# Second cross-attention of a Perceiver kernel: the context's transpose read back from DRAM, probabilities normalised ahead of transposing, context as the stationary operand, last key apart

## The reference, cut to what matters

```
def _L1_xattn_ref(queries, keys, values, mask, W_Q, W_K, W_V, W_O):
    B, S, D, H, DK, DV = (4, 256, 128, 16, 64, 64)
    b, skv, _ = keys.shape
    sq = queries.shape[1]
    scaling = 1.0 / DK ** 0.5
    Q = (queries @ W_Q).reshape(b, sq, H, DK)
    K = (keys @ W_K).reshape(b, skv, H, DK)
    V = (values @ W_V).reshape(b, skv, H, DV)
    scores = jnp.einsum('bqhd,bkhd->bhqk', Q, K)
    scores = jnp.where(mask == 0, -jnp.inf, scores)
    probs = jax.nn.softmax(scores * scaling, axis=-1)
    attn = jnp.einsum('bhqk,bkhd->bqhd', probs, V).reshape(b, sq, H * DV)
    return attn @ W_O
```

## Time and profile before

| | us |
|---|---|
| median of 3 runs | 2889.09 (2885.73 to 2889.99) |
| the profiled execution, its own time | 2895.22 |
| its span in the trace | 2893.4 |
| cross-attention 1: first query product to the last statistics | 1119.30 to 2015.25 |
| mean granted TensorE clock over the span | 0.908 of full speed |

### The profile page before, as it was taken

How to read it: one execution, slowest core, us unless ns; L and a number is a source line. 1 busy time by engine, 2 the same in 40 slices (tenths; PEclk the granted TensorE clock), 3 DMA queues, 4 the chain that set the end, 5 groups by cost and what they waited for, 6 DMA issues and landing times. The chain is left out here.

```text
span 2893.4 us, 70443 instructions
## 1 busy us (share of the span) xinstructions
PE 2370.2 (82%) x20920; PEld 1837.1 (63%) x20959; DVE 1764.7 (61%) x5309; ACT 1546.4 (53%) x3802; POOL 654.1 (23%) x1127
## 2 busy tenths in 40 slices
PE   5999999967649997999999999998256105479997
PEld 3777777745436666999999999997115103334444
DVE  5788788769844444656665666665798987521000
ACT  5888888844322224555555555554379638542221
POOL 2445454447513220111111111111000030000000
PEclk9999999989969997999999999998597655589999
DMA  3222222200000002111101011010000000010001
GB/s 89 74 75 71 73 74 74 60 3 0 19 5 0 0 0 59 32 29 29 30 27 30 27 30 30 28 27 23 13 0 0 0 0 4 0 41 0 0 0 29
DMA packets 150473, 79.92 MB, mean 28 GB/s; under 512 B 33504, under 2 KB 148592, under 8 KB 150128
## 3 DMA queue, kind: packets, MB, share of 16 engines
q1 hardware_dynamic: 150384, 78.77, 9.6%
HBM read 58.80 MB, written 19.92 MB: 27 GB/s over the span
## 5 line engine op out<-in xcount | busy, mean ns | idle before, releaser
L914 POOL TENSOR_TENSOR c_ON<-c_O,c_rden 128x512 f32<-128x512 f32 x128 | 133.4, 1042 | 718.4 <-DVE c_O L1091 718.4
L1077 DVE CUSTOM_DVE_ANT_0 c_SM<-c_bs,c_MB 128x257 f32<-128x257 f32 x512 | 215.1, 424 | 97.8 <-PE c_bs L941 95.9
L1036 ACT ACTIVATE c_OT<-c_bt 128x512 f32<-128x512 f32 x128 | 76.5, 597 | 367.2 <-PE c_bt L979 367.2
L952 PE MATMUL c_bo<-c_C,c_PT 128*128 128x128 f32 x2048 | 270.0, 275 | 0.3 <-ACT c_PT L1043 0.3
L941 PE MATMUL c_bs<-c_cT,c_QP 128*128 128x257 f32 x1024 | 266.5, 383 | 0.6 <-DVE c_cT L1059 0.5
L952 PEld LDWEIGHTS c_bo<-c_C,c_PT 128*128 128x128 f32 x2048 | 258.6, 192 | 7.3 <-ACT c_PT L1043 0.5
L666 ACT ACTIVATE a_PR<-a_SM,a_nmx 128x257 f32<-128x257 f32 x512 | 253.4, 499 | 4.0 <-issue 3.6
L1029 ACT ACTIVATE c_PR<-c_SM,c_nmx 128x257 f32<-128x257 f32 x512 | 253.6, 505 | 0.0
L713 DVE CUSTOM_DVE_ANT_0 a_SM<-a_bs,a_MB 128x257 f32<-128x257 f32 x512 | 188.0, 423 | 44.4 <-PE a_bs L534 38.5
L941 PEld LDWEIGHTS c_bs<-c_cT,c_QP 128*128 128x128 f32 x1024 | 175.9, 192 | 15.4 <-DVE c_cT L1059 0.9
L1099 DVE COPY c_PT<-c_bp 128x512 f32<-128x512 f32 x128 | 88.6, 692 | 132.8 <-PE c_bp L989 132.8
(11 more groups left out here) (479 smaller groups left out, 5722.0 us busy)
## 6 DMA issues: line engine op xcount, KB each, us to landing
a_C<-in_ctx_dram SPq DMA_DIRECT2D x128, 128.0 KB, 2.1
ctxT_dram<-a_cT SPq DMA_DIRECT2D x128, 128.0 KB, 1.9
c_C<-in_ctx_dram SPq DMA_DIRECT2D x128, 128.0 KB, 2.1
c_CL<-in_ctx_dram SPq DMA_DIRECT2D x128, 64.0 KB, 2.9
a_MK<-in_mask_Bx1xSxS_bk_dram SPq DMA_DIRECT2D x128, 32.1 KB, 1.9
X<-in_x_dram SPq DMA_DIRECT2D x4, 512.0 KB, 6.2
g_h<-in_L_ffn_h_w_dram SPq DMA_DIRECT2D x2, 1024.0 KB, 7.9
out_dram<-X SPq DMA_DIRECT2D x1, 2048.0 KB, 8.7
```

Source lines behind the costliest of these rows:

```text
L914: nc.gpsimd.tensor_tensor(ON[:, par, :, :], O1[:, :, :], bcast(rden[:, par, :], 2, D), ALU.mult).then_inc(on_ok, 1)
L952: last = nc.tensor.matmul(b_o[:, hg * D:(hg + 1) * D], PT[:, pair, i, c, :], C[:, (s.r - 2) % 8, c, :], start=(c == 0), stop=(c == 1))
L1077: nc.vector.tensor_tensor_reduce(SM[:, par, hg, :], b_s[hg % 2][:, 0:SK], MB[:, :], 1.0, NEG1, ALU.add, ALU.max, mx[:, par, hg:hg + 1]).th ...
```

## The change

- The transposed context is no longer made by TensorE and VectorE. SyncE loads it from `ctxT`, which cross-attention 0 has stored, into `cT`, now eight buffers deep, 128 KB for each element; the load of `CL` goes.
- VectorE multiplies the probabilities by the reciprocal of their sum, four instructions of 128x257 in place, ahead of the transposes. `ON`, its multiplication on GpSimd and its transposes go.
- The values are made with the context stationary and 512 columns of transposed probabilities moving: two products per element, which give the output already transposed; ScalarE copies it straight to `OT`.
- The 257th key is taken out of the values. GpSimd spreads its probabilities over a tile in `XL`; a small TensorE product with `fold` and a VectorE multiplication by `bmask` give `LT`; one more product, `LT` with `VB` (the last context rows through BH of each head), is accumulated to the output product. `VB` comes from a DRAM tensor that the preparation fills: four products of 512 columns, four ScalarE copies, one store of 1 MB.
- Scores have four banks instead of two and are issued together, ahead of the values. The small product and the output product write into spare columns of the banks `b_s[1]` and `b_s[0]`.

```
+            @block.sync
+            def _(sp):
+                sp.wait_ge(vb_ev, 4)
+                sp.dma_start(vb_dram, VBL[:, :, :]).then_inc(vb_out, 16)
+                sp.wait_ge(vb_out, 16)
...
+                pe.wait_ge(ab_ev, 8)
+                for c in range(4):
+                    wait(pe, vb_ev, c - 1)
+                    nc.tensor.matmul(b_pt[c % 2][:, :], sh.lastT[:, :], BH[:, 4 * c:4 * c + 4, :], start=True, stop=True
+                                     ).then_inc(vb_ps, 1)
...
         @block.sync
         def _(sp):
...
+            def step(s):
+                g, r = s.g, s.r
+                wait(sp, s_ps, 4 * (g - NC_ + 1))
+                sp.dma_start(cT[:, r, 0:LAST], sh.ctxT[ds(g, 1), :, :].rearrange("b d k -> d (b k)")
+                             ).then_inc(ct_in[r], 16)
+                wait(sp, av_ps, g - NC_ + 1)
                 sp.dma_start(C[:, r, :, :], ctx_rows[ds(g, 1), 0:LAST, :].rearrange("b (c p) d -> p (b c) d", p=P)
                              ).then_inc(c_in[r], 16)
-                sp.dma_start(CL[:, r, :], ctx_rows[ds(g, 1), LAST, :].broadcast_to([P, D])).then_inc(c_in[r], 16)
+                if r % 4 == 3:
+                    wait(sp, y_ps, s.tile - 1)
+                    sp.dma_start(VB[:, r // 4, :], vb_dram[ds(s.tile * BPT, BPT), :, :].rearrange("b h d -> (b h) d")
+                                 ).then_inc(vb_in[r // 4], 16)
...
# GpSimd
+                if s.on(1):
+                    wait(pool, n_ok, 4 * g)
+                    wait(pool, l_ps, s.fours(-1) - 1)
+                    nc.gpsimd.tensor_tensor(XL[:, (r - 1) // 4 % 2, (r - 1) % 4, :, :], bcast(sh.quarter[:, :], 1, 4),
+                                            PR[:, 1 - r % 2, :, LAST:SK].broadcast_to([P, 4, 4]), ALU.mult
+                                            ).then_inc(x_ok, 1)
...
# TensorE
+            def scores(s):
+                g, r = s.g, s.r
+                pe.wait_ge(ct_in[r], 16 * (s.eights(0) + 1))
+                wait(pe, last_cp, g + 1)
+                if r % 4 == 0:
+                    wait(pe, q_ev, 4 * (s.tile + 1))
+                for hg in range(4):
+                    wait(pe, s_mx, 4 * (g - 1) + hg + 1)
+                    if hg == 0 and r % 4 == 3:
+                        wait(pe, y_ev, s.fours(-7) + 1)
+                    if hg == 1 and r % 4 == 2:
+                        wait(pe, l_ev, s.fours(-6) + 1)
+                    nc.tensor.matmul(b_s[hg][:, 0:SK], QP[:, r // 4 % 2, r % 4, 4 * hg:4 * hg + 4, :], cT[:, r, :],
+                                     start=True, stop=True).then_inc(s_ps, 1)
+
+            def turn_probs(s, pair):
+                wait(pe, n_ok, 4 * (s.g - 1) + 2 * pair + 2)
+                wait(pe, (pt0_ev, pt1_ev)[pair], s.g - 1)
...
+            def values(s):
+                g, buf = s.g, (s.r - 2) % NC_
+                pe.wait_ge(c_in[buf], 16 * (s.eights(-2) + 1))
+                wait(pe, pt0_ev, g - 1)
+                wait(pe, pt1_ev, g - 1)
+                wait(pe, o_ev, g - 2)
+                for c in range(2):
+                    last = nc.tensor.matmul(b_o[:, :], C[:, buf, c, :], PT[:, s.r % 2, c, :, :],
+                                            start=(c == 0), stop=(c == 1))
+                last.then_inc(av_ps, 1)
 
             def step(s):
...
+                    scores(s)
                 if s.on(2):
+                    values(s)
                 if s.on(-4):
                     queries(s.tile + 1, r % 4)
+                if r % 4 == 1 and s.on(5):
+                    wait(pe, x_ok, 4 * s.fours(-5) + 4)
+                    if s.on(0):
+                        wait(pe, s_mx, 4 * g + 2)
+                    nc.tensor.matmul(b_s[1][0:BPT * H, SPARE:SPARE + SQ], XL[:, (r - 5) // 4 % 2, :, :, :],
+                                     sh.fold[:, :], start=True, stop=True).then_inc(l_ps, 1)
+                if r % 4 == 2 and s.on(6):
...
+                    for h in range(H):
+                        nc.tensor.matmul(b_s[0][:, SPARE:SPARE + D], OT[:, tp, h, :, :], BH[:, h, :],
+                                         start=(h == 0), stop=False)
+                    nc.tensor.matmul(b_s[0][:, SPARE:SPARE + D], LT[:, :, :], VB[:, tp, :], start=False, stop=True
+                                     ).then_inc(y_ps, 1)
                 if s.on(1):
+                    turn_probs(s, 0)
+                    turn_probs(s, 1)
...
# VectorE
                 if s.on(0):
...
                         nc.vector.tensor_tensor_reduce(SM[:, par, hg, :], b_s[hg][:, 0:SK], MB[:, :],
...
                     nc.vector.tensor_scalar(nmx[:, par, :], mx[:, par, :], -SCALE, None, ALU.mult).then_inc(s_nmx, 1)
+                if r % 4 == 1 and s.on(5):
+                    wait(dve, l_ps, s.fours(-5) + 1)
+                    wait(dve, y_ps, s.fours(-5))
+                    nc.vector.tensor_tensor(LT[:, :, :], bcast(b_s[1][0:BPT * H, SPARE:SPARE + SQ], 1, BPT),
+                                            bcast(bmask[:, :], 2, SQ), ALU.mult).then_inc(l_ev, 1)
                 if s.on(1):
+                    wait(dve, e_ok, 4 * g)
+                    nc.vector.reciprocal(rden[:, 1 - par, :], den[:, 1 - par, :]).then_inc(rd_ok, 1)
+                    wait(dve, rd_ok, g)
                     for hg in range(4):
+                        nc.vector.tensor_scalar(PR[:, 1 - par, hg, :], PR[:, 1 - par, hg, :], rden[:, 1 - par, hg:hg + 1],
+                                                None, ALU.mult).then_inc(n_ok, 1)
                     wait(dve, pt_ps, 2 * g)
+                    wait(dve, av_ps, g - 2)
+                    nc.vector.tensor_copy(PT[:, 1 - par, :, 2:4, :].rearrange("p c k q -> p c (k q)"),
+                                          b_pt[1][:, :].rearrange("p (c k) -> p c k", c=2)).then_inc(pt1_ev, 1)
+                if r % 4 == 2 and s.on(6):
+                    t = s.fours(-6)
+                    wait(dve, y_ps, t + 1)
+                    nc.vector.tensor_tensor(sh.X[:, ds(t, 1), :], sh.X[:, ds(t, 1), :],
+                                            b_s[0][:, SPARE:SPARE + D].unsqueeze(1), ALU.add).then_inc(y_ev, 1)
+                    tile_stats(nc, dve, sh, t, y_ev, t + 1)
```

More of the change, by code:

```diff
@@ L841, in _ @@
                         n += 1
+                for c in range(4):
+                    act.wait_ge(vb_ps, c + 1)
+                    nc.scalar.activation(VBL[:, 4 * c:4 * c + 4, :].rearrange("p h d -> p (h d)"), b_pt[c % 2][:, :],
+                                         ACT.Copy).then_inc(vb_ev, 1)
             @block.vector
@@ L917, in _ @@
             last_row(0, 0)
-            run(pool, step, LAGS)
+            run(pool, step, 1)
         @block.tensor
         def _(pe):
[L922 to L927, removed]
             def queries(tile, c):
                 wait(pe, q_ev, 4 * tile + c)
-                if c == 0:
-                    wait(pe, y_ev, tile - 2)
@@ new lines, in turn_probs @@
+            def turn_probs(s, pair):
+                wait(pe, n_ok, 4 * (s.g - 1) + 2 * pair + 2)
+                wait(pe, (pt0_ev, pt1_ev)[pair], s.g - 1)
+                for c in range(2):
+                    for k in range(2):
+                        last = nc.tensor.transpose(b_pt[pair][:, (2 * c + k) * P:(2 * c + k + 1) * P],
+                                                   PR[:, 1 - s.r % 2, 2 * pair + k, c * P:(c + 1) * P], sh.ident[:, :])
+                last.then_inc(pt_ps, 1)
@@ L981, in step @@
+                if s.on(2):
+                    values(s)
                 if s.on(-4):
                     queries(s.tile + 1, r % 4)
-                if s.on(1):
[L984 to L988, removed]
-                                last = nc.tensor.transpose(b_pt[pair][:, (2 * i + c) * P:(2 * i + c + 1) * P],
-                                                           PR[:, 1 - par, 2 * pair + i, c * P:(c + 1) * P],
-                                                           sh.ident[:, :])
-                        last.then_inc(pt_ps, 1)
@@ L993, in step @@
-                if r % 4 == 3 and s.on(7):
-                    wait(pe, t_ev, min(g - 3, B) if isinstance(g, int) else g - 3)
-                    if s.on(-4):
-                        wait(pe, q_ev, 4 * (s.tile + 2))
-                    else:
-                        wait(pe, y_ev, s.tile - 1)
-                    for h in range(H):
-                        last = nc.tensor.matmul(b_q[:, 0:D], OT[:, (r - 7) // 4 % 2, h, :, :], BH[:, h, :],
-                                                start=(h == 0), stop=(h == H - 1))
-                    last.then_inc(y_ps, 1)
+                if r % 4 == 1 and s.on(5):
[4 more added lines that the diff above has]
+                                     sh.fold[:, :], start=True, stop=True).then_inc(l_ps, 1)
@@ L1004, in _ @@
+                if s.on(1):
+                    turn_probs(s, 0)
+                    turn_probs(s, 1)
             for c in range(4):
                 queries(0, c)
```

(6 more changed lines are left out.)

149 lines of the change are left out of this document (54 added, 95 removed).

## The result

The changed kernel takes 2925.45 us (median of 4 runs, 2924.59 to 2928.34) against 2889.54 us before (4 runs, 2885.73 to 2896.13): ratio 1.0124, 95% interval 1.0104 to 1.0143. It is slower by 36 us; forecast were 2916 us (2898 to 2935) and 27 more. The profiled executions lie at 2925.44 and 2895.22 us, so the traces have 30 of the 36 us between them; the one of before lay 6 above its own median.

The account below looks back on a forecast made before the run. TensorE's issue time was taken to bound the stage. Steady part +20.8, start +10.3 and -0.3, end -4.7 and semaphores +1 summed to +27 us, added to the median 2889.09: 2916 us, range 2898 to 2935.

Parts of the forecast that it names:

- What bounds it: Steady second cross-attention: TensorE alone, busy 853.16 of 853.20 us; the length is the sum of what it issues.
- TensorE's own work: TensorE's period of four steps in the stage, if nothing waits: 25.23 us, 2.19 less than now.
- The normalisations: VectorE, four of 128x257 a step: 0.38 us each, 0.31 apart; ordinary steps keep 0.6 to 0.8 us spare.
- short bound: Lower limit for one VectorE normalisation, 0.30 us, from the mask product's 298 ns for 257 columns.
- long bound: Upper limit for one VectorE normalisation, 0.48 us: layer norm's 0.347 plus 129 columns at 1.06 ns.
- The two waits: TensorE idle around the turns in steps r%4 == 1, 1.54 us, and ahead of scores in r%4 == 3, 1.16 us.
- rivals A: Steady part: TensorE stays dense and neither wait shows, 2832 us; chance 0.09.
- B: Steady part: one wait alone is absent, the first (2868 us) or the second (2880 us); chance 0.06.
- Start and end: Stage's edges: +10.3 us ahead of the queries, -0.3 ahead of the first scores, -4.7 after the last scores.
- Rival D: TensorE's clock falls at the new gaps, 4 us per period at 1.2 GHz: 62 us more, 2978; chance 0.08.
- Rival C: VectorE's normalisations at or beyond the long bound: 31 x 0.42 us more, 2929; chance 0.69 together with the forecast.
- Rival E: The transposed context loads arrive late in the stage; chance 0.01, no size given.

Follow-up runs that it names:

- both moves: Changed kernel with VectorE's LT multiplication moved behind the normalisations and the addition into X moved ahead of the copy of turned probabilities: 2845.74 us, ratio 0.9836.
- extra instruction: One more 128x512 VectorE instruction per step, ahead of the reciprocal: 2937.04 us in the changed kernel, 2845.96 us in the kernel with both moves.
- Three moves of single instructions: Changed kernel, each alone: LT behind the normalisations, 2887.19 us; addition into X ahead of the copy, 2886.22; XL product ahead of the queries, 2898.88.
- the kernel with the store hidden: Kernel with both moves, the wait for the 1 MB store of VB moved from the preparation to ahead of VB's first load: 2836.77 us, ratio 0.9809.

## Why the prediction was right

**What bounds it.** Right: TensorE's slots. Taking 0.21 us of them out of each step brought 25 us.

**TensorE's own work.** The direction was right, 25.23 forecast for a dense period against 25.54 measured in the kernel with both moves. The missing 0.31 is two things, with slots elsewhere 0.01 shorter. One, 0.2, is in the seams between groups, which I had taken from the earlier trace rows without their neighbours: the queries hold 0.99 instead of 0.90 when the XL product follows (1506.36 to 1507.35), the turns 0.93 instead of 0.87 behind either small product (with both moves twice a period). The other is a third wait, which I had put at nothing. Every fourth step's scores (r mod 4 = 0) need the queries of the next tile, whose last quarter TensorE has made just ahead of the turns and ScalarE still has to copy. Kernel after, first ScalarE's copy, then TensorE's weight loads and products there:

```profile
1524.98 0.60 ACT L1026 ACTIVATE c_QP<-c_bq 128x512 f32<-128x512 f32 x1 [0.29 <-PE c_bq L946]
1525.72 1.60 PEld L962 LDWEIGHTS c_bs<-c_cT,c_QP 128*128 128x128 f32 x8
1525.72 2.00 PE L962 MATMUL c_bs<-c_cT,c_QP 128*128 128x257 f32 x8
```

The copy ends at 1525.58, and the weight load starts together with the first product at 1525.72, where in the next step it starts 0.11 ahead (1530.93 against 1531.04). The turns before it hold 0.94 instead of 0.87, the scores 1.84 instead of 1.74: about 0.16 a period, 5 us in all. Before, the output product stood between the copy and these scores. This is read from the wait in the code and these rows; no run tests it, and the profile's idle column doesn't show it. Seams and this wait make 10 us too little over 31 periods. The values came out as reckoned, 1.71 a step (1504.65 to 1506.36).

**The normalisations.** 351 ns each, 0.26 apart (1.14 for four), between my bounds of 0.30 and 0.48 and shorter than the 0.38 and 0.31 that I took. The printed length is nearer to my 0.38 than to the short bound. The extra instruction gives a slope: 417 ns for 512 columns with a constant operand against the 298 of the earlier trace rows for 257 (its input int32), 0.47 ns a column, less than half of the 1.06 that I had read from the copies for the long bound. The two elements a cycle of the Trainium skill's page "VectorE: DVE Perf Modes", section "The perf-mode tier table", put the length near the short bound of 0.30 by the prediction's estimate; measured are some 50 ns more. Whether the per-partition operand costs them, no run here shows. That ordinary steps have time to spare was right, and shown by the extra instruction.

**The two waits.** Right in place, cause and sum. First: from the end of the XL product's slot (1507.35 + 0.23) to 1508.76 are 1.18, and the turns then take 1.02 instead of 0.93, together 1.27, forecast 1.54; the shorter normalisations are most of the difference, the rest LT, which started 0.34 behind the product's start and not 0.43. Second: from 1518.21 + 0.93 to 1520.37 are 1.23, and the scores take 1.81 instead of 1.74, together 1.30, forecast 1.16. Sum 2.57 against 2.70. Three moves of single instructions, each with the size that the distances gave, leave no room for rivals A (neither wait shows) and B (one is absent).

**Start and end.** From the first scores to those of the last element it takes 2025.00 - 1140.14 = 884.9, 25.2 more than before, forecast 20.8: seams and the third wait +10, the two waits -4, and the rest, -1.2, is left for the slow start and the last steps. The start: first scores at 1140.14, before 1130.53, so 9.6, forecast 10.0 after the 0.3 that go. The end was mis-sized:

```profile
2025.00 1.97 PE L962 MATMUL c_bs<-c_cT,c_QP 128*128 128x257 f32 x8 [1.07 <-DVE X L1096]
...
2037.56 3.84 PE L1007 MATMUL c_bs<-c_B,c_OT 128*128 128x128 f32 x32 [0.46 <-ACT c_OT L1044]
2041.33 0.48 PE L1009 MATMUL c_bs<-c_VB,c_LT 64*128 64x128 f32 x2
```

That is TensorE's timeline of the kernel after at the end of the stage. The last output product ran at 2.4 GHz, 3.84 us, where I had 6.5 to 7 by the half clock that the start had shown. The end is at 2042.46, 17.5 behind the last scores; 20.3 forecast, so -7.6 instead of -4.7. The next stage starts 4.75 behind that and not 3.8, the +1 for the change-over. The stage's sum is +28, forecast +27. That it comes so near is in part luck: the +10 left out was offset by waits, start and end that were each priced too high. 2 us more lie in the last two stages, whose code is the same and whose traces I can't tell apart from two executions of one kernel.

**Rival D**, the clock falling at the new gaps: out, 1.00 over the whole steady stretch with two idle times of 1.1 to 1.2 us in every 28. The Trainium skill's page "TensorE: Matmul & The Clock Gate", section "A second HAM failure mode: psum-queue depth-cycling", describes a swing of the clock that these idle times did not bring about. The 4 us at half rate in D's price stood in no row. **Rival C** went the wrong way: the normalisations were shorter, not longer. **Rival E**: the loads landed in 2.2 us and TensorE never waited for one in the stretch.

**Where the rest is.** Traces: +30. Medians: +36. The other 6 point at the base: the profiled execution of before was 6 above its median then, and on other chips the kernel before had medians of 2893 to 2895. Against those the kernel after would be 30 to 32 slower. How much of the 36 is the base and how much the kernel, four runs of each do not settle.

## What to carry to other kernels

An engine that is idle 40% of the time can still set the pace, when a wait in its list stands ahead of work that somebody else needs first. Read the order, not the share: for each new wait write down when its producer is issued, and what is queued behind it; if a consumer is issued right behind that producer, the whole chain between them is exposed. Two moved blocks turned 1.2% slower into 1.6% faster with the same instructions.

An edit that takes a wait away can bring back more than the wait where the clock is low behind it, as the store of VB did (3.5 us of waiting, 8.2 in the stage).

When a result moves into spare columns of a bank that a faster loop uses, the loop waits for its reader; put the reader ahead of whatever it does not depend on.

## What was not expected of the hardware

- The price of an idle time can go on after it: behind 5.0 us of it the four groups of queries ran at half rate, 1.85 to 2.08 us each (granted clock 0.51), behind 1.47 us at full rate, 1.13 to 1.16 (1.00). Taking 3.5 us of waiting away gave 8.2. The length of the idle time alone does not settle it: the kernel before ran its queries at half rate (0.50) behind only 1.05 us, though the products ahead of those, 64 rows each, had run at 1.00. In the kernel with the store hidden the four products of 512 columns stand between, began below full rate (5.40 us for eight passes, granted clock 0.69) and were followed by 1.00. In three of the other kernels' traces the same product took 3.80 us at 1.00, and the queries behind their 5.0 us of idle time still ran at half rate. What tells the cases apart was not tried, and full rate behind 1.47 us is one trace.
- A group of passes can hold TensorE up to 0.1 us longer beside the small products (64 columns or 64 rows of the array), three times a period here; with the XL product moved ahead of the queries, it was the values ahead of it that held 1.82 instead of 1.71. That the shape is the cause is not shown.
